# Row sums of a softmax from ScalarE's accumulator, a new order of ScalarE's copies and exponentials, and masked queries built by GpSimd

## The chip, the core and the metric

The program runs on one core of one Trainium2 chip. The metric is the device time of one execution in microseconds (us). The kernel before took 2906.33 us, the median of three runs from 2905.99 to 2908.69.

## The reference

`reference()` computes two transformer layers over an input of 32 sequences ("batches") of 256 tokens with 128 features: an attention with relative positions beside a mixture of experts, then a second attention with causal ALiBi scores beside a second, capacity-limited mixture of experts. The change is in the first attention alone. For each batch, each of 16 heads (8 features each) and each query row:

```python
q = q / sqrt(8)
score = einsum('bhqd,bhkd->bhqk', q, k) + einsum('bhqd,qkd->bhqk', q, pe_k)   # pe_k: 129 clipped relative positions
attn  = softmax(score, axis=-1)
ctx   = einsum('bhqk,bhkd->bhqd', attn, v) + einsum('bhqk,qkd->bhqd', attn, pe_v)
return ctx @ W_out + b_out
```

So each row of exponentials must be summed over its 256 keys, and the context divided by that sum.

## The kernel before

The program has four stages one behind the other: the first mixture of experts (until about 555 us), the first attention together with the routing of the second mixture of experts (555 to 1855 us), that mixture (to about 2180 us), and the second attention. In each stage the five engines run written-out programs that meet at semaphores; nothing is reordered by a scheduler.

The first attention works in units. A unit is four heads of one half (128 queries) of one batch; a batch has `UB` = 8 units, so there are `NU0` = 256 units. All engines loop over the same steps s, one unit a step, software-pipelined. I write r for s modulo 8, and call a batch even or odd by its number, since the routing runs once for two batches.

TensorE's step s (the loop at the end of the stage) is, in this order: `turn(s-1, 0)`, four transposes of the exponentials of keys 0 to 127 (line 1025) into the single PSUM bank `probsT`; `value(s-2)`, the products of turned exponentials with the values (line 1041), and with a tile of ones (line 1045), which leaves each row's sum in the same layout as the context; `turn(s-1, 1)` for keys 128 to 255; `relative_value`, a quarter of the products with the relative values (line 1060); the scores of unit s+1 (line 1003) together with the relative scores of unit s+4 (line 1013), both into the four banks of `scores`; and last a "job", if the step has one. Jobs are what happens once in a batch: the projections `q`, `k`, `v`, the products `turn_a` and `turn_b` (line 970), which bring the relative part of the context into the layout of the context, the output projection `out`, and for the routing `xn2T`, `router1` and `prefix`. `job_list` fixes their steps, and all of them share one PSUM bank, `projected`, so each waits until the one before it has been taken out (`spare_free`).

VectorE's step s takes the least value of each negated score row while adding the bias (line 869, four instructions, each with a read of the accumulator into `low`), copies the relative scores of unit s+3 out of PSUM (`rel_s`, line 876), and then does what is due in that step: `z` (line 883, at r = 0 and 4), the context copy (line 890, r = 1), two halves of the reciprocal of the ones' products (lines 893 and 895, r = 3 and 6), the evictions of jobs, and the normalization, top-two and slot arithmetic of the routing. The scores of step s+1 wait for `rel_s` of step s, since they write the same banks.

The relative scores reach the bias through DRAM: SyncE writes `rel_s` of unit u to `rel_rows` (line 661, two transfers) and then reads unit u-1 back with a skewed pattern (line 672, two transfers). Line 869 of unit u-1 waits for that.

ScalarE's step s is: copy the first turned half of unit s-1 out of PSUM (line 751), four exponentials of unit s (line 757), copy the second turned half of unit s-1 (line 761), then jobs: `q` is four scaled and masked copies (line 730), `k` two (line 736), `xn2T` one. GpSimd has only the indirect stores of the routing's rows (line 719), each gated by a count of finished minima.

## Time and profile before

| what | value |
|---|---|
| median of three runs | 2906.33 us |
| the profiled execution | 2909.2 us, its span 2907.5 us |
| TensorE matmul, weight load | 2604.1 us (90%), 1971.0 us (68%) |
| VectorE, ScalarE, GpSimd | 1924.4 us (66%), 1611.4 us (55%), 613.6 us (21%) |
| mean granted TensorE clock | 0.969 |
| line 869, minima with bias | 1024 instructions, 373.4 us |
| line 757, exponentials | 1024 instructions, 436.8 us |
| line 1045, products with the ones | 4096 instructions, 209.6 us |

The time is the execution's, the span goes from its first to its last instruction, and 1.7 us lie around it. A matmul of fp32 operands is recorded as two instructions. Busy shares are averages over four stages, so the change has to be read from the rows of its own stage.

### The profile page before, as it was taken

How to read it: one execution, taken by the hardware profiler on the slowest of the kernel's cores; microseconds unless marked ns; L12 is line 12 of the kernel's file. 1: busy time of each engine (PE TensorE's matmuls, PEld its weight loads, DVE VectorE, ACT ScalarE, POOL GpSimd, SP SyncE). 2: the span in 40 equal slices, each digit the busy share in tenths (PEclk: the TensorE clock that was granted, in tenths of full speed). 3: DMA queues.
4: the chain of work that ended last, by engine and by line, in shares of the span. 5: the costliest groups of instructions: out<-in, count | busy, mean ns of one | idle time of the engine just before them, and what ended most of it. 6: DMA issues, size and time to landing. Idle time of an engine off the chain costs nothing. (4 is left out here: it accounts for less than half of the span.)

```text
span 2907.5 us, 102728 instructions
## 1 busy us (share of the span) xinstructions
PE 2604.1 (90%) x42000; PEld 1971.0 (68%) x42000; DVE 1924.4 (66%) x7310; ACT 1611.4 (55%) x3731; POOL 613.6 (21%) x632
## 2 busy tenths in 40 slices
PE   4999999799988999999999999499989999998998
PEld 3777777567767777777777777377766666666666
DVE  4887788467777777777777777211117777777777
ACT  1444444366666666666666665133327666767776
POOL 2445444300110000001111111400004223322230
PEclk9999999899999999999999999699999999999999
DMA  3212100166666666666666665222321001111110
GB/s 131 103 51 73 37 15 12 36 152 148 154 151 149 152 153 148 152 155 149 152 150 153 150 149 123 86 84 98 101 72 35 24 24 29 26 24 24 28 27 9
DMA packets 341502, 268.43 MB, mean 92 GB/s; under 512 B 24602, under 2 KB 328090, under 8 KB 339516
## 3 DMA queue, kind: packets, MB, share of 16 engines
q1 hardware_dynamic: 330556, 234.82, 31.4%
q0 software_dynamic: 10496, 27.28, 3.2%
q8 instruction: 323, 5.29, 0.8%
q14 instruction: 127, 1.04, 0.1%
HBM read 129.88 MB, written 132.14 MB: 90 GB/s over the span
## 5 line engine op out<-in xcount | busy, mean ns | idle before, releaser
L869 DVE CUSTOM_DVE_ANT_0 neg_scores<-scores,rel_bias 128x256 f32<-128x256 f32 x1024 | 373.4, 421 | 271.7 <-PE scores L1013 226.4
L1388 ACT ACTIVATE probs<-neg_scores,low 128x256 f32<-128x256 f32 (+1 forms) x1024 | 382.5, 446 | 211.6 <-DVE low L1419 187.4
L757 ACT ACTIVATE probs<-neg_scores,low 128x256 f32<-128x256 f32 x1024 | 436.8, 500 | 42.9 <-DVE low L869 41.8
L751 ACT COPY probsT_s<-probsT 128x512 f32<-128x512 f32 x256 | 150.3, 587 | 427.6 <-PE probsT L1025 427.6
L1419 DVE CUSTOM_DVE_ANT_0 neg_scores<-scores,alibi 128x256 f32<-128x256 f32 (+1 forms) x1024 | 304.8, 354 | 109.5 <-PE scores L1466 109.2
L1025 PE MATMUL probsT<-consts,probs 128*128 128x128 f32 x2048 | 332.7, 286 | 1.3 <-ACT probsT_s L751 0.7
L1025 PEld LDWEIGHTS probsT<-consts,probs 128*128 128x128 f32 x2048 | 229.1, 143 | 72.9 <-issue 59.4
L252 POOL TENSOR_TENSOR hid<-hid,gate_bc 128x512 f32<-128x512 f32 x160 | 205.4, 1284 | 275.8 <-DVE hid L407 257.3
L876 DVE COPY rel_s<-scores 128x768 f32<-128x768 f32 x256 | 244.0, 953 | 3.0 <-PE scores L1013 1.6
L1003 PE MATMUL scores<-k_sides,q_heads 32*128 32x256 f32 x2048 | 184.3, 429 | 55.6 <-DVE rel_s L876 54.1
L1478 PE MATMUL probsT<-consts,probs 128*128 128x128 f32 x1536 | 226.8, 285 | 3.7 <-ACT probs L1388 0.4
L1427 DVE COPY probsT_s<-probsT 128x512 f32<-128x512 f32 x256 | 175.9, 687 | 68.6 <-PE probsT L1478 68.4
L1041 PE MATMUL values<-probsT_s,v_heads 128*32 128x128 f32 x4096 | 216.1, 283 | 0.8 <-issue 0.8
L1188 ACT ACTIVATE he<-up,b1e 128x512 f32<-128x512 f32 (+1 forms) x192 | 112.0, 616 | 183.4 <-PE up L1166 183.2
L1478 PEld LDWEIGHTS probsT<-consts,probs 128*128 128x128 f32 x1536 | 172.7, 144 | 56.3 <-ACT probs L1388 39.0
L1045 PE MATMUL values<-probsT_s,ones_heads 128*32 128x128 f32 x4096 | 209.6, 276 | 0.0
L1213 DVE TENSOR_TENSOR ye<-down,b 128x512 f32<-128x512 f32 (+1 forms) x48 | 28.9, 603 | 253.0 <-PE down L1174 253.0
L712 POOL TENSOR_TENSOR scat_f<-dumpk,sk 128x8 f32<-128x8 f32 x16 | 3.1, 195 | 888.4 <-DVE dump_at L849 888.4
L275 ACT ACTIVATE th<-gate_up 128x512 f32<-128x512 f32 x160 | 95.8, 599 | 168.5 <-PE gate_up L464 166.7
L484 PE MATMUL ffn_down<-weights,hid 128*128 128x128 f32 x1280 | 184.0, 287 | 0.1
L484 PEld LDWEIGHTS ffn_down<-weights,hid 128*128 128x128 f32 x1280 | 156.8, 192 | 36.3 <-issue 27.7
L719 POOL DMA_INDIRECT packed<-xn,scat x128 | 124.2, 970 | 268.1 <-DVE low L869 243.8
(187 smaller groups left out, 5158.9 us busy)
## 6 DMA issues: line engine op xcount, KB each, us to landing
rel_rows<-rel_s SPq DMA_DIRECT2D x256, 192.0 KB
rel_bias<-rel_rows SPq DMA_DIRECT2D x256, 192.0 KB, 4.0
rel_rows<-rel_s SPq DMA_DIRECT2D x256, 128.0 KB
rel_bias<-rel_rows SPq DMA_DIRECT2D x256, 128.0 KB, 3.4
packed<-ffn_in SPq DMA_DIRECT2D x8, 1280.0 KB, 5.5
xe<-packed SPq DMA_DIRECT2D x16, 640.0 KB, 4.3
expert_out<-ye POOLq DMA_DIRECT2D x16, 640.0 KB, 6.9
xt<-xnT SPq DMA_DIRECT2D x64, 128.0 KB, 3.1
```

The lines of the kernel that those rows point to most:

```text
L252: pool.tensor_tensor(hid[p % 2][:, k, :], hid[p % 2][:, k, :], gate_bc[m % 3][:, :], ALU.mult).then_inc(hid_done, 1)
L484: ins = pe.matmul(D_ps[p % 2][:, i * D:(i + 1) * D], hid[p % 2][:, k, i * P:(i + 1) * P], wview["wdown"][:, k * D:(k + 1) * D], start=(k = ...
L757: act.activation(probs[s % 2][:, j, :], neg[s % 2][:, j, :], ACT.Exp, bias=low[s % 3][:, j:j + 1], scale=-1.0).then_inc(exped, 1)
L869: dve.tensor_tensor_reduce(neg[s % 2][:, j, :], S_ps[:, 512 * j:512 * j + S], bias_of(s)[:, j, :], 1.0, 3e38, ALU.add, ALU.min, low[s % 3] ...
L876: dve.tensor_copy(rel_s[u % 2][:, :, :], S_ps[:, :].rearrange("p (j w) -> p j w", j=4)[:, :, S:S + 3 * R]).then_inc(rel_moved, 1)
L1003: ins = pe.matmul(S_ps[:, 512 * j:512 * j + S], q_of[b % 2][rows, i, qt * P:(qt + 1) * P], k_of[b % 2][rows, qt, :], start=True, stop=True)
L1025: ins = pe.transpose(PT_ps[:, j * P:(j + 1) * P], probs[u % 2][:, j, kt * P:(kt + 1) * P], ident)
L1041: pe.matmul(O_ps[rows, qt * P:(qt + 1) * P], v_of[b % 2][:, kt, i, rows], pt[:, j, :], start=(u % UB == 0 and kt == 0), stop=(i == 3 and k ...
L1045: ins = pe.matmul(O_ps[rows, S + qt * P:S + (qt + 1) * P], one_of[:, i, :], pt[:, j, :], start=False, stop=(i == 3 and kt == KT - 1), skip ...
L1388: act.activation(probs[s % 3][:, j, 0:w], neg[s % 3][:, j, 0:w], ACT.Exp, bias=low[s % 3][:, j:j + 1], scale=-1.0).then_inc(exped, 1)
L1419: dve.tensor_tensor_reduce(neg[s % 3][:, j, 0:w], S_ps[j][:, 0:w], alibi[:, 4 * j + i, S - w:S], 1.0, 3e38, ALU.add, ALU.min, low[s % 3][: ...
L1478: ins = pe.transpose(PT_ps[kt][:, j * P:(j + 1) * P], probs[u % 3][:, j, kt * P:(kt + 1) * P], ident)
```

## The change

- The row sums no longer come from products with a tile of ones. `exps` gives each exponential instruction an accumulator output (`accum_out`), which goes into a small tile `sums`, [128 queries, 2 halves, 16 heads]. The ones, their memsets and 16 matmul records in each unit go; `ctx_s` halves.
- VectorE takes one reciprocal of a [128, 32] tile at r = 3 and copies it eightfold into `rinv_c`, where both halves of the old reciprocal were over 128 columns each. The job `turn_a` gets two more matmuls, against the identity, that turn `rinv_c` into columns 256 to 511 of `projected`. `turn_b`'s eviction multiplies by them.
- ScalarE's order becomes: exponentials 0 and 1 of unit s, copy of the first turned half of unit s-1, exponentials 2 and 3, copy of the second half. `probs` gets a third buffer.
- TensorE does `relative_value` before `turn(s-1, 1)`, not after.
- ScalarE moves the query projection out with one copy into `q_raw`; GpSimd makes the four masked and scaled queries from it (`query_heads`) under a semaphore of its own, `q_ready`. Its row stores stand in the same program now, by batch.
- `q` moves from r = 1 to r = 0, `out` from 0 to 1, and the routing's normalization is spread over other steps.

```diff
@@ -525,15 +525,17 @@
     v_of = [sm(f"v0_heads{i}", [P, KT, 4, D]) for i in range(2)]
-    one_of = sm("ones_heads0", [P, 4, 32])
     rel_s = [sm(f"rel_s{i}", [P, 4, 3 * R]) for i in range(2)]
     bias = [[sm(f"rel_bias{qt}_{i}", [P, 4, S]) for i in range(3)] for qt in range(2)]
     neg = [sm(f"neg_scores0_{i}", [P, 4, S]) for i in range(2)]
     low = [sm(f"low0_{i}", [P, 4]) for i in range(3)]
-    probs = [sm(f"probs0_{i}", [P, 4, S]) for i in range(2)]
+    probs = [sm(f"probs0_{i}", [P, 4, S]) for i in range(3)]
     probsT = sm("probsT0_s", [P, 2, 4, KT, 4, P])
-    ctx_s = sm("ctx_s", [P, 2 * S])
-    rinv = sm("rinv0", [P, S])
+    ctx_s = sm("ctx_s", [P, S])
+    sums = [sm(f"sums0_{i}", [P, 2, 4, 4]) for i in range(2)]
+    q_raw = sm("q0_raw", [P, S])
+    rinv = sm("rinv0", [P, 2, H])
+    rinv_c = sm("rinv0_c", [P, 2, H, C])
     ctx_all = sm("ctx_all", [P, S])
...
@@ -617,10 +619,10 @@
         odd = b % 2 == 1
-        if r == 0 and 2 <= b < nb + 2:
+        if r == 0 and b + 1 < nb:
+            job_list.append((s, "q", b + 1))
+        if r == 1 and 2 <= b < nb + 2:
             job_list.append((s, "out", b - 2))
-        if r == 1 and b + 1 < nb:
-            job_list.append((s, "q", b + 1))
         if r == 2 and b + 1 < nb:
...
@@ -713,12 +710,27 @@
             pool.wait_ge(rows_known, 2 * p + 2)
-            for i in range(TP):
-                for k in range(2):
-                    pool.wait_ge(lowest, 4 * min(NU0, UB * (2 * p + 5) + 2 * i + k))
-                    pool.indirect_dma_start(
-                        out=packed, out_offset=bass.IndirectOffsetOnAxis(ap=scat[:, i, k:k + 1], axis=0),
-                        in_=xn2[p % 2][:, i, :], in_offset=None).then_inc(scattered, 16)
+
+        def query_heads(b):
+            pool.wait_ge(spare_free, job_no["q", b])
+            for i in range(4):
+                ins = pool.tensor_scalar(q_of[b % 2][:, i, :], q_raw[:, :], cview["head_scale"][:, i:i + 1], q_bias[:, i:i + 1],
+                                         ALU.mult, ALU.add)
+            ins.then_inc(q_ready, 1)
+
+        query_heads(0)
+        for b in range(nb + 5):
+            if b + 1 < nb:
+                query_heads(b + 1)
+            p, odd = divmod(b - 5, 2)
+            if odd == 0 and 0 <= p < nb // 2:
+                rows_of(p)
+                for i in range(TP):
+                    for k in range(2):
+                        pool.wait_ge(lowest, 4 * min(NU0, UB * b + 2 * i + k))
+                        pool.indirect_dma_start(
+                            out=packed, out_offset=bass.IndirectOffsetOnAxis(ap=scat[:, i, k:k + 1], axis=0),
+                            in_=xn2[p % 2][:, i, :], in_offset=None).then_inc(scattered, 16)
         pool.wait_ge(scattered, 128 * (nb // 2))
...
@@ -726,10 +738,9 @@
                 act.wait_ge(spare_full, job_no[name, b])
-                for i in range(4):
-                    ins = act.activation(q_of[b % 2][:, i, :], M_ps[:, 0:S], ACT.Identity,
-                                         bias=q_bias[:, i:i + 1], scale=cview["head_scale"][:, i:i + 1])
-                ins.then_inc(spare_free, 1)
+                if b >= 1:
+                    act.wait_ge(q_ready, b)
+                act.copy(q_raw[:, :], M_ps[:, 0:S]).then_inc(spare_free, 1)
             if name == "k":
...
@@ -741,8 +752,20 @@
 
+        def exps(s, j):
+            act.wait_ge(lowest, 4 * s + j + 1)
+            act.activation(probs[s % 3][:, j, :], neg[s % 2][:, j, :], ACT.Exp, bias=low[s % 3][:, j:j + 1], scale=-1.0,
+                           accum_out=sums[s // UB % 2][:, s % UB // 4, j, s % 4:s % 4 + 1]).then_inc(exped, 1)
+
         for s in STEPS:
             u = s - 1
+            if 0 <= s < NU0:
+                if s >= 3:
+                    act.wait_ge(turned, 2 * (s - 3) + 2)
+                if s % UB == 0 and s >= 2 * UB:
+                    act.wait_ge(inverted, s // UB - 1)
+                exps(s, 0)
+                exps(s, 1)
             if 0 <= u < NU0:
...
@@ -750,12 +773,8 @@
             if 0 <= s < NU0:
-                if s >= 2:
-                    act.wait_ge(turned, 2 * (s - 2) + 2)
-                for j in range(4):
-                    act.wait_ge(lowest, 4 * s + j + 1)
-                    act.activation(probs[s % 2][:, j, :], neg[s % 2][:, j, :], ACT.Exp,
-                                   bias=low[s % 3][:, j:j + 1], scale=-1.0).then_inc(exped, 1)
+                exps(s, 2)
+                exps(s, 3)
             if 0 <= u < NU0:
...
@@ -887,17 +906,20 @@
                     dve.wait_ge(valued, UB * b)
-                    dve.tensor_copy(ctx_s[:, :], O_ps[:, :]).then_inc(ctx_moved, 1)
+                    dve.tensor_copy(ctx_s[:, :], O_ps[:, 0:S]).then_inc(ctx_moved, 1)
                 if r == 3:
-                    dve.wait_ge(ctx_moved, b)
-                    dve.reciprocal(rinv[:, 0:P], ctx_s[:, S:S + P])
-                if r == 6:
-                    link(dve.reciprocal(rinv[:, P:S], ctx_s[:, S + P:2 * S]))
+                    dve.wait_ge(exped, 4 * UB * b)
+                    link(dve.reciprocal(rinv[:, :, :], sums[(b - 1) % 2][:, :, :, :].rearrange("p t j i -> p t (j i)")))
+                    if b >= 2:
+                        dve.wait_ge(spare_full, job_no["turn_b", b - 2])
+                    dve.tensor_copy(rinv_c[:, :, :, :].rearrange("p t h c -> p (t h) c"),
+                                    rinv[:, :, :].rearrange("p t h -> p (t h)").unsqueeze(2).to_broadcast((P, 2 * H, C))
+                                    ).then_inc(inverted, 1)
             for name, b in jobs_at.get(s - 1, ()):
                 if name == "v":
                     dve.wait_ge(spare_full, job_no[name, b])
                     if b < 2:
-                        dve.wait_ge(zeros_set, 3)
+                        dve.wait_ge(zeros_set, 2)
                     else:
...
@@ -909,9 +931,9 @@
                     dve.wait_ge(spare_full, n)
-                    dve.tensor_tensor(ctx_all[:, :], M_ps[:, 0:S], ctx_s[:, 0:S], ALU.add).then_inc(spare_free, 1)
-                    dve.wait_ge(spare_free, n)
-                    dve.tensor_tensor(ctxT[:, :], ctx_all[:, :], rinv[:, :], ALU.mult).then_inc(normed, 1)
+                    dve.wait_ge(ctx_moved, b + 1)
+                    link(dve.tensor_tensor(ctx_all[:, :], M_ps[:, 0:S], ctx_s[:, :], ALU.add))
+                    dve.tensor_tensor(ctxT[:, :], ctx_all[:, :], M_ps[:, S:2 * S], ALU.mult).then_inc(spare_free, 1)
                 if name == "out":
...
@@ -925,16 +947,15 @@
             if b >= 3 and b % 2 == 1 and p < nb // 2:
-                if r == 1:
+                if r == 2:
                     normal_stats(p)
-                if r == 2:
+                if r == 3:
                     normal_begin()
-                if r == 3:
-                    newton()
-                if r == 4:
+                if r == 5:
                     newton()
                     newton()
-                if r == 5:
+                if r == 6:
+                    newton()
                     normal_end(p)
...
@@ -961,6 +982,11 @@
                 pe.wait_ge(rel_masked, 2 * b + 2)
+                if name == "turn_a":
+                    pe.wait_ge(inverted, b + 1)
+                    for qt in range(2):
+                        pe.matmul(M_ps[:, S + qt * P:S + (qt + 1) * P], rinv_c[:, qt, :, :].rearrange("p h c -> p (h c)"), ident,
+                                  start=True, stop=True)
                 where = z[:, :, :].rearrange("p t (g h q) -> p t g h q", g=8, q=4)
...
@@ -1007,7 +1033,7 @@
             if u % UB == 0:
-                pe.wait_ge(spare_free, job_no["q", b])
+                pe.wait_ge(q_ready, b + 1)
             for j in range(4):
...
@@ -1022,14 +1048,12 @@
             for j in range(4):
-                ins = pe.transpose(PT_ps[:, j * P:(j + 1) * P], probs[u % 2][:, j, kt * P:(kt + 1) * P], ident)
+                ins = pe.transpose(PT_ps[:, j * P:(j + 1) * P], probs[u % 3][:, j, kt * P:(kt + 1) * P], ident)
             ins.then_inc(turned, 1)
 
         def value(u):
             b, i, qt = u // UB, u % 4, u % UB // 4
             pe.wait_ge(moved1, u + 1)
-            if u == 0:
-                pe.wait_ge(ones_set, 4)
             if u % UB == 0:
...
@@ -1038,12 +1062,8 @@
                     rows = slice(32 * j, 32 * j + 32)
-                    pe.matmul(O_ps[rows, qt * P:(qt + 1) * P], v_of[b % 2][:, kt, i, rows], pt[:, j, :],
-                              start=(u % UB == 0 and kt == 0), stop=(i == 3 and kt == KT - 1), skip_group_check=True)
-                for j in range(4):
-                    rows = slice(32 * j, 32 * j + 32)
-                    ins = pe.matmul(O_ps[rows, S + qt * P:S + (qt + 1) * P], one_of[:, i, :], pt[:, j, :],
-                                    start=False, stop=(i == 3 and kt == KT - 1), skip_group_check=True)
+                    ins = pe.matmul(O_ps[rows, qt * P:(qt + 1) * P], v_of[b % 2][:, kt, i, rows], pt[:, j, :],
+                                    start=(u % UB == 0 and kt == 0), stop=(i == 3 and kt == KT - 1), skip_group_check=True)
             ins.then_inc(valued, 1)
...
@@ -1068,10 +1088,10 @@
                 value(s - 2)
+            if 0 <= s - 5 < NU0:
+                relative_value((s - 5) // 4, (s - 5) % 4)
             if 0 <= s - 1 < NU0:
                 turn(s - 1, 1)
-            if 0 <= s - 5 < NU0:
-                relative_value((s - 5) // 4, (s - 5) % 4)
             u, ur = s + 1, s + LEAD
```

## Rows read from the trace of the kernel before

**Rows 1.** Stretches: us, length, busy time with instructions of PE, PEld, DVE, ACT, POOL; clock; DMA
```profile
900.00:1000.00 100.00, 91.12 (x2292) 71.60 (x2295) 74.55 (x302) 62.09 (x141) 10.14 (x14) 1.00 0.60 147
1000.00:1100.00 100.00, 90.49 (x2092) 70.10 (x2087) 73.22 (x296) 62.23 (x140) 13.28 (x16) 0.97 0.61 150
```
**Rows 2.** Instructions touching the bias tile, whole run: min/median/max ns, first and last start
```profile
L869 DVE CUSTOM_DVE_ANT_0 neg_scores<-scores,rel_bias x1024: 414/420/427, 573.4 to 1804.5; 128x256 f32<-128x256 f32 x171
```
**Rows 3.** Who waited for whom, 600 to 1700 us: us in total, times, longest
```profile
ACT probsT_s L751 <- PE probsT L1025: 382.0, 228, 2.6
...
PEld projected L957 <- ACT q_heads L730: 43.8, 28, 1.7
...
DVE neg_scores L869 <- DMA rel_bias<-rel_rows: 32.8, 20, 2.8
```
**Rows 4.** TensorE in order of time: start, us, line, operation, count, idle before
```profile
1015.78 0.71 PE L1003 MATMUL scores<-k_sides,q_heads 32*128 32x256 f32 x8
...
1016.75 0.66 PE L1025 MATMUL probsT<-consts,probs 128*128 128x128 f32 x4
...
1017.58 0.40 PE L1045 MATMUL values<-probsT_s,ones_heads 128*32 128x128 f32 x8
1017.79 0.40 PE L1041 MATMUL values<-probsT_s,v_heads 128*32 128x128 f32 x8
...
1018.93 0.65 PE L1060 MATMUL relative_values<-probsT_s,rel_v 128*32 128x64 f32 x32
1020.59 0.71 PE L1003 MATMUL scores<-k_sides,q_heads 32*128 32x256 f32 x8 [1.01 <-DVE rel_s L876]
...
1021.56 1.10 PE L970 MATMUL projected<-z,consts 128*32 128x64 f32 x64
```
**Rows 5.** VectorE in order of time, steps r = 0 and 1 of an odd batch
```profile
1072.17 0.69 DVE L883 TENSOR_TENSOR z<-relative_values,consts 128x512 f32<-128x512 f32 x1 [0.68 <-PE relative_values L1060]
...
1075.27 0.42 DVE L869 CUSTOM_DVE_ANT_0 neg_scores<-scores,rel_bias 128x256 f32<-128x256 f32 x1
...
1076.65 0.95 DVE L876 COPY rel_s<-scores 128x768 f32<-128x768 f32 x1
1077.52 0.68 DVE L890 COPY ctx_s<-values 128x512 f32<-128x512 f32 x1
...
1080.51 0.42 DVE L869 CUSTOM_DVE_ANT_0 neg_scores<-scores,rel_bias 128x256 f32<-128x256 f32 x1
```
**Rows 6.** ScalarE in order of time
```profile
1075.80 1.71 ACT L757 ACTIVATE probs<-neg_scores,low 128x256 f32<-128x256 f32 x4 [0.96 <-DVE low L869]
...
1083.11 1.93 ACT L730 ACTIVATE q_heads<-projected,q_bias,consts 128x256 f32<-128x256 f32 x4
```
**Rows 7.** SyncE's transfers in order of time
```profile
684.66 1.19 SPq L661 DMA_DIRECT2D rel_rows<-rel_s  x2
685.95 1.28 SPq L672 DMA_DIRECT2D rel_bias<-rel_rows  x2
```
**Rows 8.** VectorE, the first minimum of two units that waited for their bias
```profile
678.27 0.42 DVE L869 CUSTOM_DVE_ANT_0 neg_scores<-scores,rel_bias 128x256 f32<-128x256 f32 x1 [2.54 <-DMA rel_bias<-rel_rows]
...
686.99 0.42 DVE L869 CUSTOM_DVE_ANT_0 neg_scores<-scores,rel_bias 128x256 f32<-128x256 f32 x1 [1.24 <-DMA rel_bias<-rel_rows]
```
**Rows 9.** DMA issues, 1000 to 1100 us: count, KB each, median us to landing
```profile
rel_bias<-rel_rows SPq DMA_DIRECT2D x20, 192.0 KB, 4.2
```
**Rows 10.** Groups by shape, whole run: count, busy us, mean ns, idle before
```profile
L1368 ACT COPY kT<-projected 128x256 f32<-128x256 f32 x32 | 12.0, 375 | 0.0
...
L766 ACT ACTIVATE ex<-gap 128x4 f32<-128x4 f32 x16 | 3.3, 206 | 8.4 <-DVE gap L815 8.4
...
L869 DVE DVE_READ_ACCUMULATOR2_ANT low<- 128x1 f32 x1024 | 85.4, 83 | 0.0
...
L893 DVE RECIPROCAL rinv<-ctx_s 128x128 f32<-128x128 f32 x32 | 30.2, 943 | 0.0
...
L1229 POOL TENSOR_SCALAR alibi<-consts 128x256 f32<-128x256 f32 x16 | 13.5, 848 | 1.2
```

More of the change, by code:

```diff
@@ L570, in program @@
             zeros_set = semm("zeros_set")
-            ones_set = semm("ones_set")
             started = semm("counts_cleared")
@@ L588, in program @@
             ctx_moved = semm("context_moved")
-            normed = semm("context_ready")
+            q_ready = semm("query_heads_ready")
+            inverted = semm("inverse_sums_ready")
             chain = semm("dve_chain")
@@ L702, in _, with rows_of @@
                     pool.memset(v_of[i][:, :, :, :], 0.0).then_inc(zeros_set, 1)
-                pool.memset(one_of[:, :, :], 0.0).then_inc(zeros_set, 1)
-                pool.wait_ge(zeros_set, 3)
-                for i in range(4):
-                    pool.memset(one_of[:, i, C * i:C * i + C], 1.0).then_inc(ones_set, 1)
-                for p in range(nb // 2):
+                def rows_of(p):
                     pool.wait_ge(slots_done, p + 1)
@@ L728, in move @@
                         act.wait_ge(spare_full, job_no[name, b])
-                        for i in range(4):
-                            ins = act.activation(q_of[b % 2][:, i, :], M_ps[:, 0:S], ACT.Identity,
-                                                 bias=q_bias[:, i:i + 1], scale=cview["head_scale"][:, i:i + 1])
-                        ins.then_inc(spare_free, 1)
+                        if b >= 1:
+                            act.wait_ge(q_ready, b)
+                        act.copy(q_raw[:, :], M_ps[:, 0:S]).then_inc(spare_free, 1)
                     if name == "k":
@@ L973, in project @@
                     if name == "out":
-                        pe.wait_ge(normed, b + 1)
+                        pe.wait_ge(spare_free, job_no["turn_b", b])
                         for i in range(2):
```

## The prediction

> **What bounds the kernel now.** I read the page's digits by slice first, then the stretches, the waits, and the engines in order of time within one pair of batches. Only the first attention is touched. Its 256 units run from 573.4 to 1804.5 us [rows 2], so a step takes 1231.1 / 255 = 4.83 us and a pair of batches (16 steps) 77.2 us. There TensorE is busy for 91 of 100 us, VectorE 73 to 75, ScalarE 62, at a clock of 1.00 in the one stretch and 0.97 in the next [rows 1]: the full level, 2.4 GHz, with short falls to half of it. TensorE sets the pace, not at every step. From one score start to the end of the next relative values it works without a gap from 1015.78 to 19.58 us: 3.80 us for a step with no job. The scores then wait 1.01 us for `rel_s`, so that step takes 4.81 us [rows 4]. A `turn` job's records take 1.10 us, of which 0.07 run beside what follows, so a step with one is 3.80 + 1.03 = 4.83 us [rows 4]. So the steps are of three kinds: TensorE's own work (4.2 to 4.9 us), VectorE's arithmetic (up to 5.7), and jobs that wait for ScalarE. ScalarE has slack: in 600 to 1700 us it waits 382.0 us for the first transposes, 1.7 us a step, 0.6 of it the transposes themselves [rows 3, 4].
>
> **The ones go.** Eight records start 0.21 us after the eight before them, and a unit has two such groups, so 0.43 us leave each step [rows 4]. A step with no job has 3.37 us of TensorE work. Were TensorE the bound everywhere, this alone would be 256 x 0.43 = 110 us. In exchange `turn_a` gets four records of 128 columns, priced as the transposes of the same shape, 0.55 us a batch. Its step becomes 3.37 + 1.03 + 0.55 = 4.95 us.
>
> **The query copy.** Before, four masked copies take 1.93 us [rows 6], and the next job waits for them 43.8 us in 28 batches, 1.6 us each [rows 3]. Now one copy like kT's, 0.375 us, frees the bank. On GpSimd four [128, 256] instructions of 848 ns make 3.4 us [rows 10]. They are due four steps later, over 15 us, so they are hidden. If they were exposed they would cost 3.4 us a batch, 109 us. On GpSimd's queue `query_heads` stands behind the row stores of the batch before, the last of which waits for step r = 7; `q` is made at r = 0, so nothing there is late. In odd batches it delays two stores, whose end nobody awaits within the stage. Once, at the start, GpSimd is slower than ScalarE: 3.4 + 0.4 us for 1.9, and behind its memsets; I take +2 us.
>
> **The accumulator.** No row shows it on ScalarE. Below, nothing: an added output cannot shorten the instruction. Above, a small instruction of its own, 206 ns for 4 elements, and the lost overlap of 0.07 us (four exponentials take 1.71 us, not 4 x 0.5): 0.27 us each [rows 6, 10]. VectorE's read of its accumulator is 83 ns [rows 10], the nearest row in kind, so I take a = 0.1 us each, 0.4 us a step. ScalarE then works some 3.3 us a step.
>
> **VectorE.** Two reciprocals of 0.943 us become one of [128, 32] (0.24 by its width, 0.943 at most; I take 0.35) and a broadcast copy of 256 columns (0.3, as high as 0.95 for three times that width); the context copy of 0.68 us becomes about 0.41 [rows 5, 10]. That is some 1.4 us a batch, and `z` no longer waits 0.68 us, since the relative values now end before the second transposes. The routing's work of r = 0 in an odd batch stays: from `z` at 1072.17 to the next minimum at 75.27 it is 3.1 us, which behind the 2.25 of minima and `rel_s` makes a step of 5.35 us. At r = 1, where 1077.52 to 80.51 were 3.0 us, 1.4 remain, as the context copy halves and the `out` eviction and the statistics move [rows 5].
>
> **What takes over.** Let d be the start of a unit's first minimum. Exponentials start 0.53 us later (1075.27, 1075.80) [rows 5, 6]. ScalarE's new order puts exponentials 0 and 1 ahead of the first copy, and that copy ahead of the second transposes, behind which the scores stand. So: 0.53 + 0.86 + 2a for two exponentials, 0.67 for the copy and its handover, 0.58 for the transposes: scores start at d + 2.65 + 2a, that is d + 2.85. The next minimum is 1.07 later (scores 0.97, 0.10 to VectorE): a step cannot be under 3.92 us. Before, the same loop through `rel_s` allowed about 3.6. So the reorder trades a wait for a new one, and of the 0.43 us some go back where there is no job.
>
> The second new limit is the way through DRAM. `rel_s` ends at d + 2.33 (1.38 to its start at 1076.65, then 0.95) [rows 5]. SyncE issues two writes and, 1.29 us after the first, the reads of the unit before, 0.65 us apart [rows 7]. Landing takes 4.2 us for the larger [rows 9]. Where the larger is second (r = 0 to 3) the bias is there at 2.33 + 0.05 + 1.29 + 0.65 + 4.2 = 8.5 us after d, for the unit two steps on. Two units that did wait for it, with one between, started 8.72 us apart [rows 8]. I take 8.6; where the larger is first, 8.0. So two steps may not take less, on average 4.3 us each. Before this cost 32.8 us in 1100 [rows 3], because steps were longer. It becomes common.
>
> A page of the Trainium skill, DMA: Bandwidth & Descriptors (Latency and other measured facts), gives HBM access as 0.2 us on average and 2 us at high load. This trace has landings of 4.2 us at 147 to 150 GB/s, so by that rule a faster stage would make them longer; the rival with late landings holds that without it.
>
> Sum, with jobs at 0.5 us but for the turns (and 0.9 for the router's), for an odd batch, r = 0 to 7, largest of TensorE's work, VectorE's, 3.92 and the two-step rule: 4.2, 5.35, 4.1, 4.5, 4.6, 3.92, 4.95, 4.4 = 36.0 us. The 4.6 is `v` waiting about 0.7 us for ScalarE's key copies, which now stand behind an exponential pair more. For an even batch: 4.2, 4.4, 4.2, 4.4, 4.6, 4.3, 4.95, 4.4 = 35.4. Together 71.5, with 0.9 for the clock's falls (about 1%, between the 0 and 3% of the two stretches, [rows 1]) 72.4, against 77.2. So 4.8 us a pair, 16 pairs: 77 us, less 2 at the start: 75. The profiled execution took 2909.2 us, so 2834; it was 2.9 over the median, so 2831.
>
> **A rule against it.** Four GpSimd instructions a batch now read SBUF beside VectorE. Before, GpSimd had only stores in the stage, and 1024 minima took 414 to 427 ns throughout [rows 2]; so no row shows an effect, either way. The Trainium skill, SBUF — State Buffer (Who interferes with whom), says that a VectorE instruction with two SBUF inputs and a GpSimd one that reads SBUF exclude each other for a whole instruction. The minima have one input in PSUM and would be free by it; three small slot-weight products a pair could each be held 0.85 us if they met, 16 x 2.5 = 41 us at worst, giving 2872. They are done by d + 3.6 of the step at whose end `q_raw` is filled, so they should not meet.
>
> **Rivals.** (1) The bias is not late: landings are medians of a queue that also has slack, and smoother steps may make it better. Then the bounds are 3.92 and the jobs: 34.4 + 33.3 + 0.9 = 68.6 us a pair, 138 us: 2768. For it: SyncE's issues fill only 2.5 us of a step. Against: 8.72. (2) The way through DRAM is worse: landings of 5.0, SyncE stretched, 9.4 us for two steps; the sum is 75.9 a pair, 23 us: 2884. An accumulator at its upper bound gives about 73.5 + 0.9, 2861, and lies between. For it: transfers were busy 0.61 of the stretch [rows 1] and that would rise. (3) Slower: the accumulating exponential takes twice its time, a = 0.5. The copies stand behind it, the floor becomes 4.7, and the first transposes, which need all four and the copy behind them, set 5.1 us: 16 x 5.1 + 3 = 85 us, +7.4 a pair, 118 us: 3025. It decides from a = 0.45. Against it are VectorE's 83 ns. (4) The ones were not on the path, VectorE and the bias bound all of it: within 0.2%. The unbroken TensorE rows speak against it.
>
> **Numbers.** Forecast 0.6, rival 1 0.17, rival 2 0.13, rival 3 0.05, rival 4 0.03, the rule 0.02. The time is 2831; the range takes in rival 1 and the bounds of the accumulator, 2765 to 2875. A change of under 0.2% (6 us) can't be told from none. Faster 0.92, same 0.03, slower 0.05.
>
> **What would show it.** Right: ones rows gone; the wait on the query copy under 0.3 us a batch; waits of the minima for the bias several times 32.8 us; TensorE's idle before the second transposes, put to the first copy; the floor near 3.9. Wrong: an accumulator row on ScalarE over 0.27 us; ScalarE without idle time; steps of r = 1 still over 5 us in even batches; GpSimd awaited by the relative scores.

## The result and the profile after

The changed kernel takes 2787.86 us, the median of four runs (2785.13 to 2790.77), against 2906.16 us (four runs): the ratio is 0.9591, 95% interval 0.9575 to 0.9608, so 118 us faster. 2831 was forecast, with 2765 to 2875 as range.

The profiled execution took 2785.13 us, with a span of 2783.5. Its difference to the one before is 124.0 us of span. The stage's first minimum starts 4.9 us earlier, because the stage before it happened to end 5.9 us earlier (its last eviction starts at 548.22 for 554.08 us); from first to last minimum 113.7 us are saved (1117.4 for 1231.1), and 5.4 us lie behind. So the stage itself holds 113.7 of the medians' 118 us. These rows answer to [rows 1, 2]:

```profile
900.00:1000.00 100.00, 90.41 (x2109) 72.10 (x2103) 74.64 (x304) 73.72 (x238) 17.53 (x25) 0.98 0.68 168
1000.00:1100.00 100.00, 89.96 (x2132) 71.80 (x2131) 78.98 (x336) 74.67 (x242) 12.49 (x18) 1.00 0.68 165
```

```profile
L888 DVE CUSTOM_DVE_ANT_0 neg_scores<-scores,rel_bias x1024: 418/420/426, 568.5 to 1685.9; 128x256 f32<-128x256 f32 x171
```

A step takes 1117.4 / 255 = 4.38 us for 4.83. TensorE is as busy as before, ScalarE some twelve us in a hundred busier, and the transfers' share rises from 0.61 to 0.68. The waits of 600 to 1600 us, as [rows 3] shows them for a longer stretch:

```profile
ACT probs L757 <- DVE low L888: 234.6, 203, 3.1
...
PEld probsT L1051 <- ACT probsT_s L774: 103.3, 126, 2.5
PE probsT L1051 <- ACT probsT_s L774: 82.0, 107, 2.4
DVE neg_scores L888 <- DMA rel_bias<-rel_rows: 69.6, 52, 3.4
...
PEld projected L1002 <- ACT q_raw L743: 10.6, 28, 0.4
```

Three things are to be seen. The wait of the next job on the query copy has shrunk from 43.8 us to 10.6. The wait for the bias has doubled, from 32.8 in 1100 us to 69.6 in 1000. And a new wait stands in front: TensorE's second transposes on ScalarE's first copy, line 774. PE rows are TensorE's matmuls and PEld rows its weight loads, which run beside them; what TensorE loses is read from the PE rows, 82.0 us here. TensorE in order of time, one step with a turn job, as in [rows 4]:

```profile
1016.33 0.71 PE L1029 MATMUL scores<-k_sides,q_heads 32*128 32x256 f32 x8
...
1017.30 1.10 PE L996 MATMUL projected<-z,consts 128*32 128x64 f32 x64
1018.34 0.66 PE L1051 MATMUL probsT<-consts,probs 128*128 128x128 f32 x4
1018.92 0.64 PE L1065 MATMUL values<-probsT_s,v_heads 128*32 128x128 f32 x16
1019.38 0.63 PE L1080 MATMUL relative_values<-probsT_s,rel_v 128*32 128x64 f32 x32
1019.94 0.66 PE L1051 MATMUL probsT<-consts,probs 128*128 128x128 f32 x4
1020.53 0.71 PE L1029 MATMUL scores<-k_sides,q_heads 32*128 32x256 f32 x8
```

From scores to scores it is 4.20 us, of which 1.04 are the job: 3.16 us without one. From the start of the values to the next group it is now 0.46 us (18.92 to 19.38), where values and ones had 1.02 before:

```profile
1017.33 0.42 PE L1041 MATMUL values<-probsT_s,v_heads 128*32 128x128 f32 x8
...
1018.35 0.66 PE L1025 MATMUL probsT<-consts,probs 128*128 128x128 f32 x4
```

Not all of these 0.56 us are the ones. The group that follows has changed too, since the relative values moved; e11 below tells the two apart. The accumulator, on ScalarE in order of time:

```profile
1000.95 0.51 ACT L757 ACTIVATE probs<-neg_scores,low 128x256 f32<-128x256 f32 x1 [1.39 <-DVE low L888]
1001.36 0.19 ACT L757 ACTIVATION_READ_ACCUMULATOR probs<-neg_scores,low 128x1 f32 x1
1001.46 0.49 ACT L757 ACTIVATE probs<-neg_scores,low 128x256 f32<-128x256 f32 x1
1001.86 0.19 ACT L757 ACTIVATION_READ_ACCUMULATOR probs<-neg_scores,low 128x1 f32 x1
1001.95 0.56 ACT L774 COPY probsT_s<-probsT 128x512 f32<-128x512 f32 x1
```

The read is an instruction of its own of 0.19 us, half of it beside its neighbours: the median distance from one exponential to the next is 0.49 us for 0.40 before. The other new groups, count, busy us, mean ns:

```profile
L717 POOL TENSOR_SCALAR q_heads<-q_raw,consts,q_bias 128x256 f32<-128x256 f32 x128 | 69.2, 554 | 767.2 <-ACT q_raw L743 767.1
...
L912 DVE RECIPROCAL rinv<-sums 128x32 f32<-128x32 f32 x32 | 11.0, 343 | 0.0
L915 DVE COPY rinv_c<-rinv 128x256 f32<-128x256 f32 x32 | 10.0, 312 | 1.1
```

### The profile page after: what moved, and what is told of

Read it like the earlier page. It is cut to its first block and busy times, and to the rows that moved or that the text cites. A ratio compares the mean times of both kernels' runs of the same rounds, so it can differ in the third digit from the quotient of the medians.

```text
span 2783.5 us, 95917 instructions
## 1 busy us (share of the span) xinstructions
PE 2465.6 (89%) x38032; PEld 1879.0 (68%) x38032; DVE 1877.3 (67%) x7310; ACT 1664.7 (60%) x4659; POOL 682.4 (25%) x755
## 5 line engine op out<-in xcount | busy, mean ns | idle before, releaser
L757 ACT ACTIVATE probs<-neg_scores,low 128x256 f32<-128x256 f32 x1024 | 512.1, 502 | 292.4 <-DVE low L888 276.5
L717 POOL TENSOR_SCALAR q_heads<-q_raw,consts,q_bias 128x256 f32<-128x256 f32 x128 | 69.2, 554 | 767.2 <-ACT q_raw L743 767.1
L757 ACT ACTIVATION_READ_ACCUMULATOR probs<-neg_scores,low 128x1 f32 x1024 | 192.7, 188 | 0.0
L405 DVE SCALAR_TENSOR_TENSOR ga<-th,gate_up 128x512 f32<-128x512 f32 x160 | 109.7, 686 | 96.8 <-ACT th L275 95.3
L1486 PE MATMUL scores<-kT,q_heads 32*128 32x256 f32 (+1 forms) x2048 | 165.4, 394 | 8.9 <-DVE low L1439 4.0
L1065 PE MATMUL values<-probsT_s,v_heads 128*32 128x128 f32 x4096 | 166.2, 280 | 0.7 <-ACT probsT_s L780 0.7
```

The costliest lines, as they stand in the source:

```text
L757: act.activation(probs[s % 3][:, j, :], neg[s % 2][:, j, :], ACT.Exp, bias=low[s % 3][:, j:j + 1], scale=-1.0, accum_out=sums[s // UB % 2] ...
L1486: ins = pe.matmul(S_ps[j][:, 0:w], q_of[b % 2][rows, i, q0:q0 + P], kT[b % 2][rows, 0:w], start=True, stop=True)
```

## The experiments

Each kernel was timed beside the kernel before on the same chip. e1, e2, e3 and e4 ran on a chip where that one took 2992.96 us (2977.51 to 3011.16); a_after, e6, e9 and e4b on one where it took 2903.38; e11, e12, e2b and e3b on one with 2900.26. The chips differ, so ratios are compared, and those of the first chip only with each other. Ratios do not carry over exactly either: the changed kernel has 0.9591 in the result above and 0.9635 in a_after, 13 us apart. It was not run on the third chip, so a comparison of e2b or e3b with it can be off by that much.

### e1_sums_only: the row sums alone

```diff
 # from the changed kernel, undone:
-exps(s, 0); exps(s, 1); copy of half 0; exps(s, 2); exps(s, 3)
+copy of half 0; exps(s, 0) to exps(s, 3)
-relative_value(...); turn(s - 1, 1)
+turn(s - 1, 1); relative_value(...)
-act.copy(q_raw[:, :], M_ps[:, 0:S])       # and GpSimd's query_heads
+act.activation(q_of[b % 2][:, i, :], M_ps[:, 0:S], ACT.Identity, ...)   # i = 0 to 3
 # q at r = 1, out at r = 0, the normalization's steps as before
```

> The changed kernel with all but the row sums undone: ScalarE's old order (first copy, four exponentials, second copy), relative values behind the second transposes, masked queries by ScalarE at r = 1, output job at r = 0, the routing's normalization in its old steps. Theory A (removing the ones shortens TensorE's chain; 0.56 us a step, as the values now take 0.46 us where values and ones took 1.02): it holds most of the gain, 80 to 95 us of the 118, so 2810 to 2826. Theory B (the gain is ScalarE's new order, TensorE having waited on it all along): under 40 us, 2866 or more.

Measured: 3005.6 us, ratio 1.0032 (0.9977 to 1.0087). The sums alone gave nothing. Theory A is out. The number lies on theory B's side, but its cause, ScalarE's new order, falls with e2b. Its waits, 600 to 1600 us:

```profile
PEld probsT L1047 <- ACT probsT_s L765: 81.1, 200, 1.4
PEld projected L974 <- ACT q_heads L739: 52.1, 25, 2.4
```

The first row is of weight loads. The matmuls and the copy in order of time show what TensorE lost:

```profile
1021.40 0.65 PE L1061 MATMUL values<-probsT_s,v_heads 128*32 128x128 f32 x16
1021.51 0.59 ACT L765 COPY probsT_s<-probsT 128x512 f32<-128x512 f32 x1 [1.24 <-PE probsT L1047]
1022.15 0.66 PE L1047 MATMUL probsT<-consts,probs 128*128 128x128 f32 x4
```

The second transposes start 0.05 us after the first copy's end, so they wait for it. Before, they started 0.32 us after it: the ones had covered that copy. From values to transposes it is 0.75 us for 1.01 (medians), so of the ones' 0.44 us (e11 gives this figure) 0.26 left the step and 0.18 turned into the wait. That is 67 us in 256 steps, less 20 for the inverses' four records (0.64 us a batch, see below). Why the rest does not show in the time is not told by this run alone, as the kernel before was not profiled on this chip. The wait for the queries grew from 1.6 to 2.1 us.

### e2 and e2b: ScalarE's old order

```diff
-if 0 <= s < NU0: exps(s, 0); exps(s, 1)
 act.copy(probsT[..., 0, ...], PT_ps)
-if 0 <= s < NU0: exps(s, 2); exps(s, 3)
+if 0 <= s < NU0: exps(s, 0) to exps(s, 3)
 act.copy(probsT[..., 1, ...], PT_ps)
```

> The changed kernel with ScalarE's old order alone: copy of the first turned half, then four exponentials, then the second copy. Theory A: the old order has a loop of its own (second copy 0.57, transposes 0.6, first copy 0.5, four exponentials 2.0, handovers 0.2 = 3.9 us a step), about the 3.83 us of the new one, so it costs 0 to 20 us: 2788 to 2808. Theory B: the order is the main part of the gain, 40 us or more: 2828 and up.

> The changed kernel with ScalarE's old order alone, again, on a chip where the changed kernel stands at a known ratio (0.959 to 0.964). Theory A: ratio 0.965 to 0.978, 10 to 40 us slower than the changed kernel, its steps set by the loop second copy, transposes, first copy, four exponentials. Rival (the orders are equivalent): within 0.003 of the changed kernel.

Measured: 2950.35 us on the first chip, ratio 0.9844 (0.9792 to 0.9896), with the changed kernel not beside it; 2793.26 us on the last, ratio 0.9635 (0.9614 to 0.9655). The changed kernel's ratio is 0.9635 (0.9600 to 0.9669) on the second chip and 0.9591 in the result. By the first, the rival holds and the new order is worth nothing; by the second it is worth some 13 us. The waits change their names. With the old order, TensorE waits for `rel_s`, with the new one for the first copy:

```profile
PE scores L1026 <- DVE rel_s L892: 46.8, 62, 1.7
```

### e3 and e3b: masked queries by ScalarE

```diff
-act.copy(q_raw[:, :], M_ps[:, 0:S]).then_inc(spare_free, 1)
+for i in range(4):
+    ins = act.activation(q_of[b % 2][:, i, :], M_ps[:, 0:S], ACT.Identity, bias=..., scale=...)
+ins.then_inc(spare_free, 1)
```

> The changed kernel with the four masked queries made by ScalarE again, straight from PSUM (4 x 0.48 = 1.93 us for one copy of 0.37), at r = 0. Theory A: the next job waits for them as before, 1.2 to 1.6 us a batch, 38 to 50 us: 2826 to 2838. Rival: the bias's way through DRAM and VectorE fill that time anyway, under 10 us: below 2798.

> The changed kernel with the four masked queries by ScalarE, again, beside variants on one chip. Theory A: 1.2 to 1.6 us a batch lost to the output job's wait, ratio 0.973 to 0.980. Rival (hidden behind the bias's way and VectorE): ratio below 0.967.

Measured: 2939.43 us, ratio 0.9815 (0.9755 to 0.9874), and 2837.47 us, ratio 0.9780 (0.9759 to 0.9801). Against 0.9635 the queries by GpSimd are worth 0.0145, 42 us (against 0.9591, 55), as expected in size. e2b on the same chip, with GpSimd's queries and ScalarE's old order, is 44 us faster. All of it lies in step r = 2, whose job waits for the query copies. (Step lengths here and below are mean distances from the first score matmul of a unit to that of the next, units 32 to 239, a pair of batches being 16 of them.) In this kernel the two steps r = 2 of a pair take 12.5 us, in the changed one (a_after) 8.2. On the first chip the gain does not show: e3 is not slower there than e2, which has the queries on GpSimd, ScalarE's old order and the stalls described under e9. But the price is not the wait alone. The stretch 600 to 1600 us of this kernel:

```profile
600.00:1600.00 1000.00, 870.61 (x19664) 693.34 (x19660) 721.20 (x2979) 749.29 (x2350) 97.60 (x120) 0.96 0.64 158
```

The same of the changed kernel on the second chip:

```profile
600.00:1600.00 1000.00, 890.60 (x20707) 708.02 (x20696) 752.42 (x3117) 738.42 (x2380) 159.04 (x232) 0.99 0.68 165
```

The granted clock is 0.96 for 0.99. Three hundredths of 1000 us are 30 us at most, an estimate that holds only if TensorE paced all of it; how the 42 us divide between wait and clock is not shown.

### a_after: the changed kernel again

> The changed kernel itself, unaltered, on the same chip as its variants: the kernel before took 2993 us on the chip of the first four variants, 2906 us elsewhere. Every theory: 0.955 to 0.965 of the kernel before, unless stalls like those seen in the two variants with queries by GpSimd (TensorE without instructions for some 5 us while GpSimd issues five row stores in a burst, once a pair of batches) come with this chip; then 0.97 to 0.98.

Measured: 2796.6 us, ratio 0.9635 (0.9600 to 0.9669), as expected, and without the stalls. It is the base for e6, e9 and e4b, which ran beside it.

### e6_relval_after: TensorE's old order

```diff
-relative_value((s - 5) // 4, (s - 5) % 4)
 turn(s - 1, 1)
+relative_value((s - 5) // 4, (s - 5) % 4)
```

> The changed kernel with the relative values behind the second transposes again. Theory A, mended by the first runs (without the ones, TensorE reaches the second transposes before ScalarE's first copy is done, so what they free is lost unless other work stands there): TensorE then waits 0.56 us longer for the first copy in each step it paces and the gain shrinks by 40 us or more. Rival: the relative values only change places with an idle time that is there anyway, since the loop through ScalarE sets the step: under 15 us.

Measured: 2882.14 us, ratio 0.9928 (0.9904 to 0.9952): 85 us slower than the changed kernel. Without the two moved lines, four fifths of the gain are gone. Its waits, 600 to 1600 us:

```profile
PE probsT L1051 <- ACT probsT_s L774: 125.7, 146, 2.6
...
DVE z L902 <- PE relative_values L1080: 59.8, 53, 1.4
```

The same wait in a_after:

```profile
PE probsT L1051 <- ACT probsT_s L774: 85.4, 107, 2.3
```

Theory A holds: the wait for the first copy grows, and `z` waits 1.1 us each time. The size has a simple reason. In ScalarE's new order the next scores come after minimum, two exponentials, first copy and second transposes. In the changed kernel the smallest distance of two `rel_s` copies is 3.83 us. Here the relative values stand within that loop, between transposes and scores, and the smallest distance is 4.42 us, 0.59 more; from their start to that of the scores it is 0.58. More than half of all steps lie within 0.13 us of this new floor, and a pair takes 76.2 us for 70.7.

### e9_spread_stores: GpSimd's stores two steps later

```diff
-pool.wait_ge(lowest, 4 * min(NU0, UB * b + 2 * i + k))
+pool.wait_ge(lowest, 4 * min(NU0, UB * b + 2 + 2 * i + k))
```

> The changed kernel with each of GpSimd's eight row stores of a pair gated two steps later, so that none comes in a burst behind the query copies. Theory A (the burst, with SyncE's transfers, keeps TensorE's instructions from arriving): on a chip that shows the stalls of 5 us, they go, 16 x 5 to 8 us with the clock's fall behind them: 60 us or more faster than the unaltered one; on a chip without them, within 8 us. Rival (the stalls are the chip's own): no difference on either.

Measured: 2791.69 us, ratio 0.9620 (0.9587 to 0.9652), 5 us under the changed kernel and inside the interval, as both theories have it for a chip without stalls. This chip had none, so they were not told apart. It came from e2 on the first chip, GpSimd and TensorE in order of time:

```profile
1058.18 1.05 POOL L731 DMA_INDIRECT packed<-xn,scat  x1 [0.53 <-POOL scat L711]
1059.54 0.97 POOL L731 DMA_INDIRECT packed<-xn,scat  x1 [0.30 <-issue]
1060.82 0.97 POOL L731 DMA_INDIRECT packed<-xn,scat  x1 [0.31 <-issue]
```

```profile
1063.57 0.22 PE L1077 MATMUL relative_values<-probsT_s,rel_v 128*32 128x64 f32 x1 [1.35 <-issue]
1065.00 0.27 PE L1077 MATMUL relative_values<-probsT_s,rel_v 128*32 128x64 f32 x1 [1.21 <-issue]
```

TensorE had nothing to wait for that the profile shows, for 4 us in all, in the middle of a group of matmuls, while GpSimd issued its burst (1058.18 to 1064.34 us). What holds it there stays open.

### e4 and e4b: the bias one step more ahead

```diff
-LEAD = 4
+LEAD = 5
```

> The changed kernel with the relative scores one unit further ahead of the scores (LEAD 5 for 4), so that the bias has three steps instead of two for its way through DRAM. Theory A: this way is the second limit; the minima's waits for the bias (69.6 us in 1000) go and half of them comes back as time: 30 to 45 us, 2743 to 2758, with the share of 3.83 us steps rising. Rival: the loop through ScalarE's first copy takes their place, under 10 us gained: 2778 or more.

> The changed kernel with LEAD 5 for 4, as before, now beside the unaltered changed kernel. Theory A: 30 to 45 us faster than it, as the minima's waits for the bias go. Rival: the loop through ScalarE's first copy takes their place, under 10 us.

Measured: 2929.11 us, ratio 0.9784 (0.9736 to 0.9833), on the first chip; 2748.31 us, ratio 0.9467 (0.9435 to 0.9499), on the second: 48 us faster than the changed kernel, a little more than theory A's 45, and the fastest of all. This wait of a_after is gone:

```profile
DVE neg_scores L888 <- DMA rel_bias<-rel_rows: 62.1, 45, 2.5
```

What leads now:

```profile
DVE neg_scores L888 <- PE scores L1039: 170.0, 179, 2.5
PEld probsT L1051 <- ACT probsT_s L774: 66.3, 111, 1.8
```

### e11 and e12: the move alone, and with the sums

e11 is the kernel before with `relative_value` ahead of `turn(s - 1, 1)`; e12 is e1 with that same move.

> The kernel before with one edit: the relative values ahead of the second transposes. Theory A (the move only matters once the ones are gone, since values and ones together, 1.02 us, cover ScalarE's first copy of 0.6 us): VectorE's z starts 0.6 us earlier twice a batch, of which some shows; 0 to 20 us faster than before, ratio 0.993 to 1.000. Rival (the move is a gain of its own, the 85 us that undoing it cost): ratio below 0.98.

> The kernel before with the accumulator's row sums and the relative values ahead of the second transposes, and nothing else of the change (ScalarE's old order, its masked queries, the old job steps). Theory A (sums alone gave a ratio of 1.003, the move makes room for them): 50 to 80 us faster than before, ratio 0.972 to 0.983. Rival (the new order of ScalarE is needed as well): ratio above 0.99.

Measured: e11 2868.56 us, ratio 0.9887 (0.9866 to 0.9908), 32 us faster than before; e12 2873.32 us, ratio 0.9898 (0.9871 to 0.9924). e11 lies between its theories. e12 misses theory A and stands at the edge of its rival, whose cause, ScalarE's new order, e2b does not bear out.

e11 first. The move is worth 32 us without any other part of the change, more than theory A allowed. Its rows show the ones' real size:

```profile
1004.07 0.43 PE L1041 MATMUL values<-probsT_s,v_heads 128*32 128x128 f32 x8
...
1004.97 0.63 PE L1060 MATMUL relative_values<-probsT_s,rel_v 128*32 128x64 f32 x32
```

Values with ones take 0.90 us up to the relative values, 0.46 without ones in the changed kernel: the ones are 0.44 us. Up to the second transposes, as in the kernel before, it was 1.01, though these waited for no one: the copy had ended 0.32 us earlier. The move takes this gap of 0.11 us away. The three groups values, relative values and second transposes take 2.18 us in the kernel before (medians, from start to start up to the scores), 2.05 in e11, 1.61 in the changed kernel. So the move makes TensorE's own step 0.13 us shorter, which in 256 steps is 33 us, the size of e11's gain; `z`'s wait for the relative values also fell, from 48.4 to 18.5 us in 600 to 1600 us. What the gap is that goes, no run shows.

e12 against e11 is the sums alone, on one chip: 5 us slower, within the noise. TensorE has 0.44 us less in each step and 0.64 us more in a batch for the inverses, so 5.8 us less in a pair. ScalarE's part grew meanwhile, by 0.09 us for each exponential, and TensorE waits for it longer. The wait for the query copies, e11's row and then e12's, 600 to 1600 us, and the two stretches:

```profile
PE projected L957 <- ACT q_heads L730: 35.0, 27, 1.6
```

```profile
PE projected L974 <- ACT q_heads L739: 49.2, 26, 2.4
```

```profile
600.00:1600.00 1000.00, 909.99 (x22729) 746.67 (x22724) 748.64 (x2943) 647.82 (x1464) 94.68 (x117) 0.99 0.64 156
```

```profile
600.00:1600.00 1000.00, 864.56 (x19328) 685.13 (x19328) 703.12 (x2909) 720.41 (x2308) 91.24 (x114) 0.96 0.63 154
```

The two steps r = 3 of a pair, behind the query copies, take 13.6 us in e12 and 11.2 in e11; the other fourteen are 1.8 us shorter together. So the other steps return a third of the 5.8 us, and this place takes it back. e12 there, TensorE first and then the stretches:

```profile
1070.24 0.71 PE L1025 MATMUL scores<-k_sides,q_heads 32*128 32x256 f32 x8 [1.37 <-DVE rel_s L890]
...
1072.71 1.22 PE L974 MATMUL projected<-xt,weights 128*128 128x256 f32 x2 [1.42 <-ACT q_heads L739]
1073.72 1.06 PE L1047 MATMUL probsT<-consts,probs 128*128 128x128 f32 x4
1074.71 1.08 PE L1061 MATMUL values<-probsT_s,v_heads 128*32 128x128 f32 x16
1075.57 1.08 PE L1076 MATMUL relative_values<-probsT_s,rel_v 128*32 128x64 f32 x32
```

```profile
1066.00:1072.00 6.00, 3.92 (x81) 2.92 (x74) 5.24 (x28) 4.30 (x13) 1.99 (x3) 0.97 0.64 163
1072.00:1078.00 6.00, 5.29 (x62) 4.12 (x66) 2.72 (x12) 3.48 (x12) 0.97 (x1) 0.50 0.73 165
```

After two waits in a row, of 1.37 and 1.42 us, the clock falls from 2.4 to 1.2 GHz (0.97, then 0.50), and the values take 0.86 us (1074.71 to 75.57) for 0.46. An estimate of where the 5.8 us went: TensorE's waits (the PE rows of `--waits`, 600 to 1600 us) add up to 135 us for e11's 89, of the 46 more 40 for ScalarE, which is 3.5 us a pair of 76; and 0.03 of the clock are 2.3 us at most. Together they can be the whole of it; they were not changed one at a time.

Two things are left untested. The kernel with everything but the sums was not run, so what the sums are worth in the full change is not shown. Nor were the new steps of `q`, `out` and the routing's normalization run by themselves. e12 and e3b, on one chip, differ by these and by ScalarE's order: 2873.32 and 2837.47 us, 36 us, of which ScalarE's order has some 13 at most by e2b, if it counts the same there.

## Why the prediction was right, and where it was not

**What bounds, and the sign.** Right in sign, and right step by step. The changed kernel's steps, r = 0 to 7 (means as under e3), are 4.2, 5.3, 4.2, 4.2, 4.5, 4.2, 4.9, 4.2 us in an odd batch and 4.1, 4.3, 3.9, 4.7, 4.4, 4.2, 4.8, 4.2 in an even one: 70.3 us a pair, each within 0.35 us of its entry in the prediction's sum, 71.5. The largest are those that it names, VectorE's work and the turns. But what is taken from TensorE does not always come back: e1 and e12 took the ones out and gained nothing.

**The ones.** The 0.43 us is right (0.44 by e11). The step without a job is 3.16 us, not 3.37, for two other reasons: the 3.80 us that it starts from hold 0.07 that run beside the next group, and a gap of 0.11 us goes with the move. The larger error is in what the ones are worth. They were booked as a gain of TensorE's own path, limited only by two later rules. e1 and e12 show them worth nothing while ScalarE makes the queries.

**The step of it that failed: TensorE's new order has no term.** The prediction mentions the relative values' move for `z`, which "no longer waits 0.68 us" (right: 8.4 us in 1000 for 48.4). Without saying so it also builds on the move in its floor of 3.92, which counts only the transposes between the first copy and the scores. It never priced the move itself. Undoing it costs 85 us (e6), as the floor then is 4.42 us, and alone it gives 32 (e11).

**Where the 43 us between forecast and result lie.** The steps came out at 70.1 us a pair over the whole stage (1117.4 x 16 / 255), against 72.4: 16 pairs by 2.3 us are 37. Of the 2.3, 0.9 were added for the clock's falls, which the measured steps already contain, and the rest is spread over all steps. The comparison is also not of like with like: the sum is for a pair with routing work, while the 77.2 us that it was subtracted from are a mean over the stage. Pairs with routing took 78.1 us before. So the result lies in the range in part by luck: its lower end was set for rival 1, not for any of these.

**ScalarE's new order.** "Trades a wait for a new one": right, and e2b shows the trade at 0 to some 13 us. The floor of 3.92 us came out at 3.83 as the smallest distance of `rel_s` copies.

**The accumulator.** a = 0.1 us was taken between 0 and 0.27; 0.09 was measured. The reciprocal (0.35 forecast, 0.343), the broadcast (0.3, 0.312) and the context copy (0.41, 0.414) came as priced; the inverses' four records took 0.64 us of TensorE for 0.55.

**The query copy.** Right in mechanism: 1.6 us a batch became 0.4 (under 0.3 was named as the sign of being right), and the whole part is worth 42 us (e3b) where 1.2 to 1.6 us a batch would be 38 to 51. The clock, which the prediction left at the same 0.9 us a pair in both kernels, is part of that. GpSimd's instructions take 554 ns, not the 848 of the row that they were priced by, and are nowhere waited for except once at the start; there the stage begins 0.9 us later instead of 2 (first minimum 20.3 us after the last eviction of the stage before, for 19.4).

**The way through DRAM.** Right as the second limit, which e4b shows with 48 us, and in size: the 56 units whose first minimum waited for its bias started a median 8.6 us after the unit two before, as forecast. As a fixed limit it was a little too strict, since the shortest such distance is 8.1 us. Landings are shorter on the whole, 3.5 us for the larger reads where the page before has 4.0 and the one stretch read had 4.2:

```profile
rel_bias<-rel_rows SPq DMA_DIRECT2D x256, 192.0 KB, 3.5
...
rel_bias<-rel_rows SPq DMA_DIRECT2D x256, 128.0 KB, 3.0
```

The Trainium skill's rule (DMA: Bandwidth & Descriptors, Latency and other measured facts), by which more load means later landings, isn't borne out here: 165 to 168 GB/s instead of 147 to 150 [rows 1], and no later landings. Whether steadier steps outweighed the load, as rival 1 has it, no run separates.

**The rule on shared access.** The minima still take 418 to 426 ns, and so do the 124 of them that ran beside GpSimd's query instructions. This agrees with the Trainium skill, SBUF — State Buffer (Who interferes with whom), on an instruction with at most one input in SBUF. The slot-weight products, for which a loss was priced, never met GpSimd's query instructions, as the prediction expected (166 to 168 ns at the last of them); so the loss itself was not tested.

**The rivals.** Rival 1 (bias never late) missed in its condition, as waits for the bias doubled. But what it argued from, shorter landings, did come, and the result is nearer to its 2768 us than to 2831. Rival 2 (later still) missed; its own sum also gives 19 us and 2887, not 23 and 2884, as the 2 us at the start were added instead of taken off. Rival 1's leaves these 2 us out. Rival 3 falls with the accumulator's 0.09 us, rival 4 with the result.

## What to carry to other kernels

Work taken off the engine that sets the pace is only worth what does not turn into a wait at the next handover: look which copy the removed work had covered, and whether another engine's part grew in exchange. Price a pure change of order like any other edit: by the loop that the moved work enters or leaves, and by what the groups beside it take from start to start. Undo parts from the changed kernel as well as adding them to the old one; here the two ways gave 85 and 32 us for the same two lines, as the moved work lies within the loop that sets the floor in ScalarE's new order (4.42 us for 3.83) and not in that of the old one (3.58 us in the kernel before and in e11).

## What the runs showed of the hardware

- An exponential with an accumulator output on ScalarE is followed by a read of 188 ns, which lengthens the distance between exponentials by only 0.09 us (median distance 0.49 for 0.40 us).
- A masked and biased [128, 256] fp32 copy from SBUF took GpSimd 554 ns, 848 ns for the other `tensor_scalar` of the same size in the stage after.
- TensorE took 0.90 us from the start of values and ones to matmuls of the same 128*32 form, and 1.01 us to transposes (128*128) that waited for nothing the profile shows.
- The granted clock of one stage was 0.96 for 0.99 when TensorE waited for four copies by ScalarE once a batch, with less work than in the kernel before between those waits (e3b, e12). In e1, which has both as well, it was 0.98.
- The kernel before took 2993 us on one chip and 2900 to 2906 us in the other comparisons.
